# Quantiser's last periods on VectorE, and stage four's first quarter begun inside stage three

## The chip, the cores and the metric

One core of a Trainium2 chip runs the whole program. The metric is the device time of one execution in microseconds, the median over several runs. Every other time here comes from one profiled execution of the kernel.

## What is computed

The input `x` has shape (16, 32, 32, 32). Four stages follow each other, each adds to `x` a function of the normalised `x` (`_gn`: mean and variance over the 32x32 pixels of one channel):

```python
x = x + _L0_conv_ref(_gn(x), codebooks)      # residual quantiser: 8 codebooks of 512 rows of 32
x = x + _L1_conv_ref(_gn(x), ...)            # 1x1 and 3x3 convolutions, products of 8x8 patch spectra
x = x + _L2_conv_ref(_gn(x), ...)            # four directional scans, 31 dependent steps each
x = x + _L3_conv_ref(_gn(x), ...)            # snake convolution: offsets, sampling, normalisation
```

The two that the change touches, in short:

```python
def stage(res, cb):                          # quantiser, one codebook
    d = sum(res * res) - 2.0 * einsum('ne,ke->nk', res, cb) + sum(cb * cb)
    q = cb[argmin(d)]
    return (res - q, q)
...
off = conv2d(x, w_off, b_off, (1, 1), 'SAME')          # snake convolution, 3x3, 18 offsets
off = tanh(group_norm(off, g_gn_off, b_gn_off, K))
y_off_new = running sums of off outwards from the centre
out = conv2d(bilinear samples of x at y + y_off_new, w_dsc, ...)
out = relu(group_norm(out, g_gn, b_gn, 8))
```

## The kernel before

`x` stays in SBUF for the whole program as `X`, 128 partitions (four images x 32 channels) x 4 quarters of 1024 pixels. A quarter is `j`; half a quarter (512 columns) is a unit. Each stage is one function (`block_l0` to `block_l3`) that writes out the program of each engine by hand, with semaphores between engines. A stage ends in a barrier of all engines. Ahead of each stage stands a small block of its own, `prime`, in which SyncE (SP) increments every semaphore of the stage once (so that waits can be written as `START + n` with `START = 1`); a second barrier ends it.

**The quantiser, `block_l0`.** There are 64 periods: 8 codebooks x 8 units, and 5 more periods in which the pipeline drains. For one period's unit: TensorE (PE) scores the codebook, VectorE (DVE) finds the best row (`find`, line 553, an index per pixel), the index is spread over partitions (PE L268, then ScalarE's cast `l_ib`, L391), GpSimd (POOL) and ScalarE (ACT) turn it into one-hot rows: of the 8 one-hots of a unit (four groups `g`, near and far chunk) POOL makes the four near ones (`near`, L444) and one far one (L467), ACT the other three (L358, L364). PE picks the row and its step with them (L277, bank `PICK`). DVE adds it to the residual (`l_res`, L579), POOL multiplies by the step (`l_product`, L479), PE sums (L325), ACT takes a sign (L397), POOL multiplies sign and step (`l_signed`, L453) and subtracts it from the residual (`l_res`, L461). `back(w, i, par, n)` names the unit that is `n` periods behind: `early` 1, `fresh` 2, `mid` 3, `done` 5. When all is drained DVE takes the eight residuals out of `X` (L590). The text below numbers the units of the last codebook 59 to 63 by their period.

**Stage three's end, `block_l2`.** After the last scan step PE moves the result back in two halves (L1083), and DVE adds it to `X` in eight instructions (L1185): four give the pixels of quarters 0 and 1, four those of quarters 2 and 3. SP has loaded stage four's weights long before.

**Stage four's beginning, `block_l3`.** DVE takes statistics of quarter 0 (L1625, L1628, L1630), writes it normalised into `l_xz` (padded rows) and once more into `l_xe` (L1634), and then does the same for quarters 1 to 3. SP gathers the shifted columns for the offset convolution: for a quarter 12 DMAs from SBUF to SBUF, each 32 partitions x 1154 columns (`l_xi`, L1307). PE runs the offset convolution of both halves (24 matmuls each half, L1336) in one bank, between them ACT copies the first half out (`l_raw`, L1478); DVE takes its moments (L1640, L1643), ACT the tanh (L1490), and ACT and DVE split the offsets in turn into three 16-bit parts (L1493, L1671, L1497, L1677, L1503). With them PE forms running sums (L1354), from which DVE makes the first `l_term` (L1705), and POOL adds terms (`l_isum`, L1609) for the rest of the stage. Meanwhile POOL makes `l_down` and `l_bend` of quarter 0 (L1588, L1593).

## Time and profile before

| | us |
|---|---|
| median of 3 runs | 1644.4 (1643.44 to 1646.78) |
| the profiled execution | 1646.22 |
| its span, first to last instruction | 1643.3 |
| PE, POOL, DVE, ACT busy | 1389.7, 1076.4, 1240.0, 977.5 |
| stage one ends, stage two begins | 882.4, 884.9 |
| stage two ends, stage three begins | 1116.1, 1118.1 |
| stage three ends, stage four begins | 1311.5, 1314.15 |

The last three rows are places on the span's time axis, which all times of the trace use. A stage's end is the end of its last arithmetic, a stage's beginning the start of the first instruction behind both barriers. The profiled execution takes 2.9 us more than its span; what lies outside the span is no part of the trace.

### The profile page before, as it was taken

Reading aid. Unit: us, or ns where it says so; the run is one execution under the profiler, and the core shown is the slowest. Engines: PE = TensorE matmul, PEld = TensorE weight load, DVE = VectorE, ACT = ScalarE, POOL = GpSimd, SP = SyncE. Lnnn points to the kernel's source line nnn. Section 1 sums busy time; section 2 is a strip of 40 time slices with the busy share of each in tenths; the row PEclk is TensorE's granted clock in tenths of the full one; section 3 lists DMA queues with packets and bytes.
Section 4 is the critical chain, followed back from the end, with each engine's and each line's share of the span. In section 5 each row is a group of like instructions: output and inputs, shape, how many; then the busy total and the mean of one; then the engine's idle time right before and its main releaser. Section 6 shows DMA issues by size and latency. Waiting matters only on the chain. (4 is left out here: it accounts for less than half of the span.)

```text
span 1643.3 us, 36454 instructions
## 1 busy us (share of the span) xinstructions
PE 1389.7 (85%) x11793; PEld 605.9 (37%) x11812; DVE 1240.0 (75%) x4975; ACT 977.5 (59%) x1652; POOL 1076.4 (66%) x783
## 2 busy tenths in 40 slices
PE   3999999999999999999982999985888738676675
PEld 1333333333333333333331777753656401111111
DVE  4899999999999899999975354444222357877786
ACT  2488888888888788888881444321000025656554
POOL 4579999989999899999994223232000049788786
PEclk9999999999999999999996999997999958897877
DMA  7000000000000000000002435501000031010000
GB/s 166 8 2 9 5 9 4 2 11 5 9 4 2 11 5 9 4 2 2 1 2 57 98 83 115 115 0 53 1 2 2 1 87 44 1 44 14 1 14 26
DMA packets 18468, 42.27 MB, mean 26 GB/s; under 512 B 6501, under 2 KB 8137, under 8 KB 18269
## 3 DMA queue, kind: packets, MB, share of 16 engines
q1 hardware_dynamic: 16540, 38.50, 10.4%
q8 instruction: 97, 1.59, 0.4%
q10 hardware_dynamic: 1728, 1.35, 0.4%
q14 instruction: 103, 0.84, 0.2%
HBM read 8.92 MB, written 2.10 MB: 7 GB/s over the span
## 5 line engine op out<-in xcount | busy, mean ns | idle before, releaser
L444 POOL TENSOR_SCALAR l_onehot<-l_ib,c_iota 128x512 bf16<-128x512 f16 x256 | 400.6, 1565 | 58.3 <-ACT l_ib L391 58.3
L553 DVE FIND_INDEX8 l_idx<-l_top,l_scored 128x8 uint32<-128x256 f32 x1024 | 419.7, 436 | 0.0
L254 PE MATMUL ps<-l_ct_slot,l_res 32*128 32x512 f32 x2048 | 411.6, 613 | 0.0
L570 DVE CUSTOM_DVE_ANT_0 l_scored<-ps,l_gain 128x256 f32<-128x256 f32 x1024 | 383.8, 432 | 18.4 <-ACT l_gain L373 17.5
L373 ACT ACTIVATE l_gain<-ps 128x768 f32<-128x768 f32 (+1 forms) x384 | 284.2, 740 | 117.2 <-PE ps L254 116.6
L1609 POOL TENSOR_TENSOR l_isum<-l_term 128x512 f32<-128x512 f32 x160 | 205.1, 1313 | 65.9 <-DVE l_term L1711 34.5
L277 PE MATMUL ps<-l_onehot,l_cbp_slot 128*32 128x512 bf16 x3072 | 214.6, 386 | 6.6 <-POOL l_onehot L444 3.3
L248 PE MATMUL ps<-l_csq,l_row_slot 32*128 32x512 bf16 x1024 | 155.3, 397 | 17.9 <-DVE l_csq L548 6.4
L1362 PE MATMUL ps<-l_isum,w_l_w_dsc 64*64 64x512 f32 x640 | 104.8, 723 | 69.8 <-POOL l_isum L1609 68.9
L254 PEld LDWEIGHTS ps<-l_ct_slot,l_res 32*128 32x128 f32 x2048 | 155.9, 194 | 11.7 <-issue 0.9
L1537 ACT ACTIVATE ps<-ps,w_l_minus 128x512 f32<-128x512 f32 x192 | 118.3, 663 | 67.3 <-DVE l_term L1711 50.2
L730 PE MATMUL ps<-l_wc,l_xi 100*128 100x192 f32 x768 | 133.5, 331 | 24.5 <-DMA l_xi<-l_xt 24.5
L391 ACT CAST l_ib<-ps 128x512 f16<-128x512 f32 x256 | 149.3, 583 | 0.0
L730 PEld LDWEIGHTS ps<-l_wc,l_xi 100*128 100x128 f32 x768 | 125.9, 192 | 37.5 <-issue 36.7
L358 ACT ACTIVATE l_away<-l_ib,c_minus_iota 128x512 f16<-128x512 f16 x192 | 139.6, 727 | 0.0
L364 ACT ACTIVATE l_onehot<-l_away,c_one 128x512 bf16<-128x512 f16 x192 | 138.9, 723 | 0.0
L268 PEld LDWEIGHTS ps<-c_ident,l_idx 128*128 128x128 f16 x1024 | 58.8, 99 | 200.6 <-ACT l_ib L391 140.5
L1711 DVE SCALAR_TENSOR_TENSOR l_term<-ps,l_bend 128x512 f32<-128x512 f32 x192 | 120.4, 682 | 11.7 <-ACT ps L1537 11.4
L1584 POOL COPY l_xe<-l_xe 128x128 f32<-128x128 f32 (+1 forms) x16 | 6.2, 422 | 184.4 <-DVE l_xe L1634 184.2
L277 PEld LDWEIGHTS ps<-l_onehot,l_cbp_slot 128*32 128x32 bf16 x3072 | 59.2, 95 | 148.3 <-issue 59.9
L248 PEld LDWEIGHTS ps<-l_csq,l_row_slot 32*128 32x128 bf16 x1024 | 37.7, 91 | 192.7 <-DVE l_top L570 102.2
L268 PE MATMUL ps<-c_ident,l_idx 128*128 128x128 f16 x1024 | 103.3, 224 | 2.0 <-ACT l_idx L387 1.3
(157 smaller groups left out, 1955.5 us busy)
## 6 DMA issues: line engine op xcount, KB each, us to landing
l_xi<-l_xt SPq DMA_DIRECT2D x48, 384.0 KB, 7.0
l_xi<-l_xz SPq DMA_DIRECT2D x48, 144.2 KB, 3.1
X<-in_x SPq DMA_DIRECT2D x16, 128.0 KB, 7.9
out<-X SPq DMA_DIRECT2D x16, 128.0 KB, 2.1
l_ct<-in_codes_t SPq DMA_DIRECT2D x4, 448.0 KB, 13.0
l_ct_slot<-l_ct SPq DMA_DIRECT2D x7, 256.0 KB, 2.3
l_cbp_slot<-l_cbp SPq DMA_DIRECT2D x8, 96.0 KB, 1.9
l_wt<-in_l_w SPq DMA_DIRECT2D x1, 768.0 KB, 3.9
```

Source lines behind the costliest of these rows:

```text
L248: pe.matmul(ps[:, at + n - FIRST[k], :], row_slot[rows, par, :], csq[rows, :], start=True, stop=False, skip_group_check=True)
L254: pe.matmul(ps[:, at + n - FIRST[k], :], res[rows, i, P * tt:P * (tt + 1)], ct_slot[rows, par, :], start=False, stop=True, skip_group_chec ...
L268: mm = pe.matmul(ps[:, SPREAD, P * tt:P * (tt + 1)], idx16[:, i % 2, n:n + 1].to_broadcast([P, P]), ident16[:], start=True, stop=True)
L277: mm = pe.matmul(ps[C * g:C * g + C, PICK, :], cbp_slot[:, par, kind, a, c, :], onehot[:, i % 2, g, c, :], start=(c == 0 and a == 0), stop ...
L358: nc.scalar.activation(away[:, n, :], ib16[:, i % 2, g, :], ACT.Abs, bias=minus_iota[:, 1:2]).then_inc(s_away, 1)
L373: nc.scalar.activation(gain[:, at:at + GROUPS[k], :], ps[:, at:at + GROUPS[k], PAIRED:], ACT.Relu).then_inc(s_gain, 1)
L391: nc.scalar.copy(ib16[:, vi % 2, k - 2, :], ps[:, SPREAD, :]).then_inc(s_ib, 1)
L444: nc.gpsimd.tensor_scalar(onehot[:, i % 2, g, 0, :], ib16[:, i % 2, g, :], iota[:, 0:1], None, ALU.is_equal).then_inc(s_near, 1)
L553: nc.vector.max_index(idx8[:, i % 2, n, :], top[:, i % 2, n:n + 1].to_broadcast([P, 8]), scored[:, WIDE * (k % 3) + n - FIRST[k], :]).then ...
L570: nc.vector.tensor_tensor_reduce(out=scored[:, WIDE * (k % 3) + m, :], in0=ps[:, WIDE * (k % 2) + m, :PAIRED], in1=gain[:, WIDE * (k % 2) ...
L730: mm = pe.matmul(ps[:, py % 2, HID * u:HID * (u + 1)], xi[:, ky, g, at:at + P], wc[:, ky, :], start=(ky == 0), stop=(ky == 2))
L1609: nc.gpsimd.tensor_tensor(isum[:, it % SUMS, :], term[:, t0, :], term[:, t0 + 1, :], ALU.add).then_inc(s_sum, 1)
```

## The change

1. **Drain of the quantiser.** POOL and ACT's one-hots leave the last five periods. DVE runs a new function `drain` there: it makes the remaining one-hots of unit 62 (six) and unit 63 (eight), and does the three POOL operations (`settle`: sign times step, residual minus that; and the product), with the removal of each residual from `X` (`leave`) put between. A new semaphore `s_last` counts DVE's one-hots.
2. **No `prime`** ahead of stages three and four: their semaphores count from zero, one barrier is left of two. Stages one and two keep theirs, and stage one has one semaphore more to prime.
3. **Quarter 0 of stage four is normalised in stage three**: after the four adds of the first half DVE takes its statistics and writes `l_xz`, with the other four adds around it, and SP issues its gather at the end of its program of stage three.
4. **The gather by halves**: every quarter's gather has 24 DMAs, 12 of 612 columns for the upper half of the convolution (semaphore `s_xi[0]`), then 12 of 542 for the lower.
5. **First quarter by halves in stage four**: the convolution's second half goes to another bank (`ACC`), and tanh, rounding and splitting run as two pieces of 512 columns. The copy `l_xe` of quarter 0 is made first in stage four, then the other quarters.

```diff
+LATE_HOTS = (G - 2 + G, G - 2 + G + 2 * G)
...
+                        if scoring or w == ALL:
+                            pe.wait_ge(s_near, START + v * G + G)
+                        else:
+                            pe.wait_ge(s_near, START + (ALL - 2) * G + 2)
+                            pe.wait_ge(s_last, START + LATE_HOTS[v - (ALL - 2)])
...
-            periods(pool, period, DRAIN)
+            periods(pool, period, 0)
...
-            periods(dve, period, DRAIN)
-            for i in range(UNITS):
+            def hot(v, i, g, c):
+
+                dve.wait_ge(s_ib, START + v * G + (g + 1))
+                nc.vector.tensor_scalar(onehot[:, i % 2, g, c, :], ib16[:, i % 2, g, :], iota[:, c:c + 1], None,
+                                        ALU.is_equal).then_inc(s_last, 1)
+
+            def settle(v, i):
+
+                dve.wait_ge(s_sign, START + v + 1)
+                nc.vector.tensor_tensor(signed[:], signed[:], step[:, i % KEPT, :], ALU.mult).then_inc(s_signed, 1)
+                dve.wait_ge(s_signed, START + v + 1)
+                nc.vector.tensor_tensor(res[:, i, :], res[:, i, :], signed[:], ALU.subtract).then_inc(s_res, 1)
+
+            def leave(i):
+
                 dve.wait_ge(s_res, START + ALL + i + 1)
                 xi = X[:, i * HALF:(i + 1) * HALF]
                 nc.vector.tensor_tensor(xi, xi, res[:, i, :], ALU.subtract).then_inc(s_out, 1)
+
+            def drain(w, i, scoring, par, use):
+                if scoring:
+                    return period(w, i, scoring, par, use)
+                early, fresh, mid, done = (back(w, i, par, n) for n in (1, 2, 3, 5))
+                if early:
+                    dve.wait_ge(s_top, START + early[0] * TILES + TILES)
+                    dve.sem_inc(s_alone, 1)
+                    find(early[1], SLOTS - 1)
+                if fresh:
+                    v, vi, vp = fresh
+                    for g in range(2 if early else 0, G):
+                        hot(v, vi, g, 0)
+                    for g in range(G):
+                        hot(v, vi, g, 1)
+                if done:
+                    settle(done[0], done[1])
+                if i == 0:
+                    for e in range(UNITS - DRAIN):
+                        leave(e)
+                if mid:
+                    v, vi, vp = mid
+                    dve.wait_ge(s_middle, START + v + 1)
+                    nc.vector.tensor_tensor(res[:, vi, :], res[:, vi, :], ps[:, PICK, :],
+                                            ALU.add).then_inc(s_off, 1)
+                    dve.wait_ge(s_off, START + v + 1)
+                    dve.wait_ge(s_product, START + v)
+                    nc.vector.tensor_tensor(product[:, vi % 2, :], res[:, vi, :], step[:, vi % KEPT, :],
+                                            ALU.mult).then_inc(s_product, 1)
+                if done:
+                    leave(done[1])
+
+            periods(dve, drain, DRAIN)
...
+def load_columns(sp, xz, xi, j, s_xi):
+
+    flat = xz[:, j].rearrange("p y x -> p (y x)")
+    for h, at in enumerate((slice(0, UPPER), slice(UPPER, SHIFTED))):
+        for g in range(G):
+            for kx in range(3):
+                sp.dma_start(xi[C * kx:C * kx + C, g, at],
+                             flat[C * g:C * g + C, kx + at.start:kx + at.stop]).then_inc(s_xi[h], 16)
...
-        prime(nc, semaphores)
...
+            sp.wait_ge(s_zero, START + 1)
+            sp.wait_ge(s_next_xz, START + 1)
+            load_columns(sp, xz, xi, 0, s_xi)
...
+            act.wait_ge(s_next, START + 3)
+            nc.scalar.activation(xstd[:, 0:1], xmv[:, 0:1, 1], ACT.Sqrt, bias=eps[:]).then_inc(s_next_std, 1)
...
+            for r in range(G):
+                add_output(0, r)
+            dve.wait_ge(s_out, START + G)
+            for h in range(2):
+                nc.vector.bn_stats(xstats[:, 0, h, :], X[:, h * HALF:(h + 1) * HALF]).then_inc(s_next, 1)
+            dve.wait_ge(s_next, START + 2)
+            nc.vector.bn_aggr(xmv[:, 0, :], xstats[:, 0]).then_inc(s_next, 1)
+            add_output(1, 0)
+            dve.wait_ge(s_next_std, START + 1)
+            nc.vector.reciprocal(xrstd[:, 0:1], xstd[:, 0:1]).then_inc(s_next, 1)
+            dve.wait_ge(s_next, START + 4)
+            dve.wait_ge(s_zero, START + 1)
+            nc.vector.tensor_scalar(xz[:, 0, 1:H + 1, 1:W + 1], X[:, 0:HW].rearrange("p (y x) -> p y x", x=W),
+                                    xmv[:, 0, 0:1], xrstd[:, 0:1], ALU.subtract, ALU.mult).then_inc(s_next_xz, 1)
+            for r in range(1, G):
+                add_output(1, r)
...
-            for j in range(J):
-                columns(j)
+            for j in range(1, J):
+                sp.wait_ge(s_xz, START + j)
+                sp.wait_ge(s_conv, START + 2 * j)
+                load_columns(sp, xz, xi, j, s_xi)
...
-                    if ky == 0 and h == 0:
-                        pe.wait_ge(s_xi, START + (j + 1) * (16 * 3 * G))
+                    if ky == 0:
+                        pe.wait_ge(s_xi[h], (j + 1) * (16 * 3 * G))
...
-            for h in range(2):
-                if h:
-                    pe.wait_ge(s_raw[0], START + h)
-                offset_conv(0, h, range(3))
+            offset_conv(0, 0, range(3))
+            offset_conv(0, 1, range(3), ACC)
...
+            halves = [slice(HALF * h, HALF * (h + 1)) for h in range(2)]
+            for at in halves:
+                nc.scalar.activation(off[:, at], raw[:, 0, at], ACT.Tanh, bias=gstat[:, 0, 5:6],
+                                     scale=gstat[:, 0, 4:5]).then_inc(s_first_rounded, 1)
+            for h, at in enumerate(halves):
+                act.wait_ge(s_first_rounded, START + h + 1)
+                nc.scalar.copy(rounded[:, at], off[:, at]).then_inc(s_first_rounded, 1)
...
+            normalise(0, xe[:, 0, MID:MID + H, MID:MID + W], s_xe)
+            for j in range(1, J):
+                for h in range(2):
+                    at = j * HW + h * HALF
+                    nc.vector.bn_stats(xstats[:, j, h, :], X[:, at:at + HALF]).then_inc(s_gn, 1)
+            dve.wait_ge(s_gn, START + 2 * (J - 1))
+            for j in range(1, J):
+                nc.vector.bn_aggr(xmv[:, j, :], xstats[:, j]).then_inc(s_gn, 1)
+            dve.wait_ge(s_std, START + 1)
+            nc.vector.reciprocal(rstd[:, 1:], std[:, 1:]).then_inc(s_gn, 1)
+            dve.wait_ge(s_gn, START + 3 * (J - 1) + 1)
+            for j in range(1, J):
+                normalise(j, xz[:, j, 1:H + 1, 1:W + 1], s_xz)
+                normalise(j, xe[:, j, MID:MID + H, MID:MID + W], s_xe)
```

Where instructions stand, before and after, at the three places that matter. First VectorE at the end of stage one; before, behind the last search:

```order
L553 MAX_INDEX l_idx<-l_top,l_scored 128x8 x4
L579 TENSOR_TENSOR l_res<-l_res,ps 128x512 x3
L590 TENSOR_TENSOR X<-X,l_res 128x512 x8
L74 UNCONDITIONAL_BRANCH
```

and VectorE there after the change (`L596` a one-hot, `L602` and `L604` the two operations of `settle`, `L610` a `leave`, `L634` the add of before's L579, `L638` the product):

```order
L560 MAX_INDEX l_idx<-l_top,l_scored 128x8 x4
L596 TENSOR_SCALAR l_onehot<-l_ib,c_iota 128x512 x6
L602 TENSOR_TENSOR l_signed<-l_signed,l_step 128x512
L604 TENSOR_TENSOR l_res<-l_res,l_signed 128x512
L610 TENSOR_TENSOR X<-X,l_res 128x512 x3
L634 TENSOR_TENSOR l_res<-l_res,ps 128x512
L638 TENSOR_TENSOR l_product<-l_res,l_step 128x512
L610 TENSOR_TENSOR X<-X,l_res 128x512
L596 TENSOR_SCALAR l_onehot<-l_ib,c_iota 128x512 x8
L602 TENSOR_TENSOR l_signed<-l_signed,l_step 128x512
L604 TENSOR_TENSOR l_res<-l_res,l_signed 128x512
L634 TENSOR_TENSOR l_res<-l_res,ps 128x512
```

The first add behind the search now stands behind six one-hots, a `settle` and three `leave`s; the second behind eight more one-hots and a `settle`. Next VectorE from the end of stage three into stage four, before:

```order
L1185 TENSOR_TENSOR X<-X,ps 128x16x32 x8
L989 UNCONDITIONAL_BRANCH
L1618 UNCONDITIONAL_BRANCH
L1625 BN_STATS l_xstats<-X 128x6 x2
L1628 BN_AGGR l_xmv<-l_xstats 128x2
L1630 RECIPROCAL l_rstd<-l_std 128x1
L1634 TENSOR_SCALAR l_xz<-X,l_xmv,l_rstd 128x32x32
L1634 TENSOR_SCALAR l_xe<-X,l_xmv,l_rstd 128x32x32
L1625 BN_STATS l_xstats<-X 128x6 x6
```

and the same place on VectorE after the change:

```order
L1253 TENSOR_TENSOR X<-X,ps 128x16x32 x4
L1259 BN_STATS l_xstats<-X 128x6 x2
L1261 BN_AGGR l_xmv<-l_xstats 128x2
L1253 TENSOR_TENSOR X<-X,ps 128x16x32
L1264 RECIPROCAL l_rstd<-l_std 128x1
L1267 TENSOR_SCALAR l_xz<-X,l_xmv,l_rstd 128x32x32
L1253 TENSOR_TENSOR X<-X,ps 128x16x32 x3
L1054 UNCONDITIONAL_BRANCH
L1695 UNCONDITIONAL_BRANCH
L1699 TENSOR_SCALAR l_xe<-X,l_xmv,l_rstd 128x32x32
L1706 BN_STATS l_xstats<-X 128x6 x6
```

Statistics and `l_xz` of quarter 0 moved ahead of the stage's barrier (the branches); `l_xe` and all of the other quarters stay behind it. Last SyncE over the same border, before (the second and third branch lead through the priming block):

```order
L1064 DMA w_l_stack<-in_l_stack 128x64
L989 UNCONDITIONAL_BRANCH
L57 UNCONDITIONAL_BRANCH
L56 UNCONDITIONAL_BRANCH
L1297 UNCONDITIONAL_BRANCH
L1307 DMA l_xi<-l_xz 32x1154 x48
L1315 DMA out<-X 32x1024 x16
```

and SyncE after the change:

```order
L1128 DMA w_l_stack<-in_l_stack 128x64
L1040 DMA l_xi<-l_xz 32x612 x12
L1040 DMA l_xi<-l_xz 32x542 x12
L1054 UNCONDITIONAL_BRANCH
L1376 UNCONDITIONAL_BRANCH
L1040 DMA l_xi<-l_xz 32x612 x12
L1040 DMA l_xi<-l_xz 32x542 x12
```

All 24 DMAs of quarter 0 now stand ahead of SyncE's branch, and so ahead of the barrier that ends stage three.

## Rows read from the trace of the kernel before

**Rows 1.** Chain that ended last, share of the span by line (page).

```profile
POOL l_isum L1609 10%; PE ps L1362 1%; PE ps L1336 1%; SPq L1307 0%; POOL l_bend L1593 0%; POOL l_down L1588 0%; DMA l_xi<-l_xz 0%; POOL X L1616 0%; PE ps L1324 0%; ACT l_raw L1478 0%; PE ps L1385 0%; DVE l_term L1705 0%; DVE l_term L1711 0%; DVE l_stats L1640 0%
```

**Rows 2.** Timeline, 848 to 886 us: start, duration, engine, line, [idle before, releaser].

```profile
851.12 0.43 DVE L553 FIND_INDEX8 l_idx<-l_top,l_scored 128x8 uint32<-128x256 f32 x1
...
856.49 0.69 ACT L397 ACTIVATE l_signed<-ps,c_minus_tiny 128x512 f32<-128x512 f32 x1 [0.30 <-PE ps L325]
...
861.02 0.69 DVE L579 TENSOR_TENSOR l_res<-l_res,ps 128x512 f32<-128x512 f32 x1 [6.17 <-PE ps L277]
...
864.75 0.69 ACT L397 ACTIVATE l_signed<-ps,c_minus_tiny 128x512 f32<-128x512 f32 x1 [2.72 <-POOL l_res L461]
...
866.25 1.47 PE L277 MATMUL ps<-l_onehot,l_cbp_slot 128*32 128x512 bf16 x12 [3.31 <-POOL l_onehot L444]
...
871.58 0.69 DVE L579 TENSOR_TENSOR l_res<-l_res,ps 128x512 f32<-128x512 f32 x1 [9.87 <-PE ps L277]
872.18 10.26 DVE L590 TENSOR_TENSOR X<-X,l_res 128x512 f32<-128x512 f32 x8
...
873.55 0.69 ACT L397 ACTIVATE l_signed<-ps,c_minus_tiny 128x512 f32<-128x512 f32 x1 [3.55 <-PE ps L325]
...
877.44 0.69 ACT L397 ACTIVATE l_signed<-ps,c_minus_tiny 128x512 f32<-128x512 f32 x1 [3.21 <-POOL l_res L461]
```

**Rows 3.** Line 444 alone, POOL's near one-hots: min/median/max ns, first and last start.

```profile
L444 POOL TENSOR_SCALAR l_onehot<-l_ib,c_iota x256: 1552/1564/1581, 69.9 to 864.6; 128x512 bf16<-128x512 f16 x128
```

**Rows 4.** Two lines of VectorE alone, the same columns.

```profile
L514 DVE TENSOR_SCALAR l_res<-X,l_mv,l_rstd x8: 529/544/830, 26.2 to 63.0; 128x512 f32<-128x512 f32 x8
```

```profile
L541 DVE CAST l_csq<-l_csq_left x1: 427/427/427, 25.7 to 25.7; 128x512 bf16<-128x512 f32 x1
```

**Rows 5.** SyncE's own barrier instructions between stages two and three, the same columns.

```profile
L617 SPq EVENT_SEMAPHORE  x1: 17/17/17, 1116.5 to 1116.5; - x1
```

```profile
L56 SPq EVENT_SEMAPHORE  x1: 17/17/17, 1118.0 to 1118.0; - x1
```

**Rows 6.** Timeline, 1303 to 1353 us, columns as in rows 2.

```profile
1302.71 0.35 DVE L1167 SCALAR_TENSOR_TENSOR l_columns<-ps,l_bias,l_columns 128x128 f32<-128x128 f32 x1 [0.98 <-PE ps L1105]
...
1306.63 4.87 DVE L1185 TENSOR_TENSOR X<-X,ps 128x512 f32<-128x512 f32 x8 [2.24 <-PE ps L1083]
1314.15 1.29 DVE L1625 BATCH_NORM_STATS2 l_xstats<-X 128x6 f32<-128x512 f32 x2 [2.65 <-PEq L56]
...
1316.24 0.81 DVE L1634 TENSOR_SCALAR l_xz<-X,l_xmv,l_rstd 128x1024 f32<-128x1024 f32 x1
1316.97 0.81 DVE L1634 TENSOR_SCALAR l_xe<-X,l_xmv,l_rstd 128x1024 f32<-128x1024 f32 x1
...
1327.26 5.35 PE L1336 MATMUL ps<-l_xi,w_l_w_off 96*32 96x512 f32 x24 [18.76 <-DMA l_xi<-l_xz]
...
1329.01 0.81 DVE L1634 TENSOR_SCALAR l_xe<-X,l_xmv,l_rstd 128x1024 f32<-128x1024 f32 x1
...
1339.60 0.21 DVE L1643 BATCH_NORM_AGGREGATE l_mv<-l_stats 128x2 f32<-128x12 f32 x1
...
1343.32 1.24 ACT L1490 ACTIVATE l_off<-l_raw,l_gstat 128x1024 f32<-128x1024 f32 x1
...
1351.28 1.89 DVE L1705 SCALAR_TENSOR_TENSOR l_term<-ps,l_down 128x512 f32<-128x512 f32 x3 [1.93 <-remote]
```

**Rows 7.** Chain of waits, 1300 to 1353 us, first and last gather of quarter 0 (start, duration).

```profile
1317.08 0.59 SPq L1307
...
1324.14 3.08 DMA l_xi<-l_xz
```

**Rows 8.** SyncE's other DMA issues, by line, columns as in rows 3.

```profile
L215 SPq DMA_DIRECT2D l_row_slot<-l_stage_row x7: 602/602/723, 70.5 to 647.9; - x7
```

```profile
L703 SPq DMA_DIRECT2D l_xi<-l_xt x48: 591/1910/2056, 891.7 to 1055.8; - x48
```

```profile
L201 SPq DMA_DIRECT2D l_cbp_slot<-l_cbp x8: 464/465/592, 31.5 to 682.0; - x8
```

More of the change, by code:

```diff
@@ L398, in period @@
                                              bias=const["minus_tiny"][:]).then_inc(s_sign, 1)
-                    if fresh:
+                    if fresh and scoring:
                         v, vi, vp = fresh
@@ L978, with block_l2 @@
 DIRS = 4
-def block_l2(nc, ps, X, io, const, w3, xz):
+def load_columns(sp, xz, xi, j, s_xi):
[5 more added lines that the diff above has]
+                             flat[C * g:C * g + C, kx + at.start:kx + at.stop]).then_inc(s_xi[h], 16)
+def block_l2(nc, ps, X, io, const, w3, ahead, s_xi):
+    START = 0
     ident, eps = const["ident"], const["eps"]
+    xz, xi, xstats, xmv, xstd, xrstd = (ahead[name] for name in ("xz", "xi", "xstats", "xmv", "std", "rstd"))
     with ExitStack() as ctx:
@@ L1179, in _, with add_output @@
                 scan(d, step)
-            for half in range(2):
+            def add_output(half, r):
                 dve.wait_ge(s_turned, START + 4 + half + 1)
-                for r in range(G):
-                    xj = X[:, HW * 2 * half:HW * (2 * half + 2)].rearrange("p (j y r x) -> p r j y x", j=2, r=G, x=W)
-                    src = ps[:, 2 * r + half, :].rearrange("p (j y x) -> p j y x", j=2, x=W)
-                    nc.vector.tensor_tensor(xj[:, r], xj[:, r], src, ALU.add).then_inc(s_out, 1)
+                xj = X[:, HW * 2 * half:HW * (2 * half + 2)].rearrange("p (j y r x) -> p r j y x", j=2, r=G, x=W)
+                z = ps[:, 2 * r + half, :].rearrange("p (j y x) -> p j y x", j=2, x=W)
+                nc.vector.tensor_tensor(xj[:, r], xj[:, r], z, ALU.add).then_inc(s_out, 1)
+            for r in range(G):
[14 more added lines that the diff above has]
+                add_output(1, r)
             dve.wait_ge(s_out, START + 2 * G)
@@ L1213, with block_l3 @@
 SHIFTED = (H + 2) * PADW - 2
+UPPER = (ROWS + 2) * PADW
 OWN = ((0, 1), (2, 3), (4, 5), (6, 7), (8,))
 L3_WEIGHTS = ("l3_w_off", "l3_avg", "l3_cols", "l3_sums", "l3_part_mask", "l3_minus", "l3_w_dsc", "l3_stack")
-def block_l3(nc, ps, X, io, const, w3, xz, out):
+def block_l3(nc, ps, X, io, const, w3, ahead, s_xi, out):
+    START = 0
     eps = const["eps"]
+    xz, xi, xstats, xmv, std, rstd = (ahead[name] for name in ("xz", "xi", "xstats", "xmv", "std", "rstd"))
     with ExitStack() as ctx:
@@ L1462, in _ @@
         def _(act):
-            for i, js in enumerate((range(1), range(1, J))):
-                act.wait_ge(s_gn[i], START + 3 * len(js))
-                nc.scalar.activation(std[:, js.start:js.stop], xmv[:, js.start:js.stop, 1], ACT.Sqrt,
-                                     bias=eps[:]).then_inc(s_std, 1)
+            act.wait_ge(s_gn, START + 3 * (J - 1))
+            nc.scalar.activation(std[:, 1:], xmv[:, 1:, 1], ACT.Sqrt, bias=eps[:]).then_inc(s_std, 1)
             nc.scalar.copy(ones[:], sums[:]).then_inc(s_ones, 1)
@@ L1477, in copy_raw @@
                         act.wait_ge(s_y, START + j)
-                nc.scalar.activation(raw[:, norm, HALF * h:HALF * (h + 1)], ps[:, SIDE, :], ACT.Identity,
+                bank = ACC if norm == 0 and j == 0 and h == 1 else SIDE
+                nc.scalar.activation(raw[:, norm, HALF * h:HALF * (h + 1)], ps[:, bank, :], ACT.Identity,
                                      bias=cols[:, 3 * norm:3 * norm + 1]).then_inc(s_raw[norm], 1)
@@ L1521, in _ @@
             group_std(0, 0)
-            offsets(0)
-            middle_part(0)
-            all_parts(0)
+            act.wait_ge(s_gs[0], START + GS)
+            halves = [slice(HALF * h, HALF * (h + 1)) for h in range(2)]
[5 more added lines that the diff above has]
+                nc.scalar.copy(rounded[:, at], off[:, at]).then_inc(s_first_rounded, 1)
+            for h, at in enumerate(halves):
+                act.wait_ge(s_first_left, START + h + 1)
+                nc.scalar.copy(rounded[:, at], left[:, at]).then_inc(s_first_rounded, 1)
+            for h, at in enumerate(halves):
+                act.wait_ge(s_first_left, START + h + 3)
+                nc.scalar.copy(parts[:, 0, at], off[:, at]).then_inc(s_off, 1)
             for p in range(PASSES):
@@ L1683, in _ @@
             gain_of(0, 0)
-            first_left(0)
-            second_left(0)
+            halves = [slice(HALF * h, HALF * (h + 1)) for h in range(2)]
+            for a, (src, dst) in enumerate(((off, left), (left, off))):
+                for h, at in enumerate(halves):
+                    dve.wait_ge(s_first_rounded, START + 2 * a + h + 3)
+                    nc.vector.scalar_tensor_tensor(out=dst[:, at], in0=rounded[:, at], scalar=part_mask[:, a:a + 1],
+                                                   in1=src[:, at], op0=ALU.mult, op1=ALU.add).then_inc(s_first_left, 1)
             for p in range(PASSES):
@@ L1882, in build_program @@
         w3 = {name: t("w_" + name, list(io[name].shape), F32) for name in L3_WEIGHTS}
-        xz = t("l3_xz", [P, J, H + 2, PADW])
-        block_l2(nc, ps, X, io, const, w3, xz)
-        block_l3(nc, ps, X, io, const, w3, xz, out)
+        ahead = {"xz": t("l3_xz", [P, J, H + 2, PADW]), "xi": t("l3_xi", [3 * C, G, (H + 2) * PADW]),
+                 "xstats": t("l3_xstats", [P, J, 2, 6]), "xmv": t("l3_xmv", [P, J, 2]),
+                 "std": t("l3_std", [P, J]), "rstd": t("l3_rstd", [P, J])}
+        s_xi = [ctx.enter_context(nc.semaphore("l3_xi_" + name)) for name in ("upper", "lower")]
+        block_l2(nc, ps, X, io, const, w3, ahead, s_xi)
+        block_l3(nc, ps, X, io, const, w3, ahead, s_xi, out)
 def kernel(**inputs):
```

77 lines of the change are left out of this document (25 added, 52 removed).

## Prediction

> **What bounds the kernel now.** I read the chain that ended last first: only its tail is kept, the running sums of stage four on POOL [rows 1]. The change touches nothing of that tail; it moves the point from which it starts. A kernel of four stages with barriers is bounded stage by stage, so I went to the three borders that the diff touches and read the timeline there.
>
> *End of stage one.* The last search ends at 851.55; from there the drain is a chain through POOL. Sign(60) ends at 857.18, the add of unit 62 starts 3.84 us later at 861.02 after an idle of 6.17, sign(61) comes at 864.75 because POOL's `l_res` was late, PE's picks of unit 63 at 866.25 because a POOL one-hot was late, so the add of unit 63 starts at 871.58 after 9.87 us without work on DVE [rows 2]. A POOL one-hot takes 1.56 us [rows 3]. Behind the add DVE takes eight residuals out of `X` in 10.26 us, of which the last waits for unit 63 (sign(63) at 877.44); the end is 882.44 [rows 2]. DVE, the idle engine, could do the same work: that is what the edit does.
>
> *Between stages two and three* the first barrier releases SP at 1116.5 and the second at 1118.0 [rows 5]: 1.5 us go into the priming block.
>
> *Stage three to four.* The eight adds run 1306.63 to 1311.50, statistics start 1314.15, `l_xz` is done at 1317.05. PE's first convolution waits for the gather, 18.76 us of idle ending at 1327.26; DVE meanwhile runs from `l_xe` of quarter 0 (1316.97) to the last `l_xe` (1329.82), 12.85 us. Moments are aggregated at 1339.60, tanh starts at 1343.32, the first term at 1351.28 [rows 6]. The gather is 12 issues from 1317.08 to 1324.14, 0.642 us apart, and the last lands 3.08 us behind its issue [rows 7].
>
> **The change part by part.** The profiled execution took 1646.22 with a span of 1643.3, 1.8 us over the median of the runs; I work out the change of the span and apply it to the median.
>
> *1. The drain.* New on DVE: 14 one-hots, and per unit two operations of `settle` and a product. An f32 tensor-tensor takes 0.69 [rows 2], taken as 0.70 with its wait; adds follow each other at 0.61 [rows 6], taken as 0.60 for a `leave`. DVE shows no one-hot (f16 in, bf16 out, a scalar per partition). The nearest rows: a 128x512 f32 tensor_scalar 0.544, a 128x512 cast into bf16 0.427 [rows 4]. Successive tensor_scalars start 0.08 closer than their length (0.81 long, 0.73 apart [rows 6]), so 0.46 and 0.35 apart; I take 0.40. Then: search ends 851.55; six one-hots to 853.95; settle(59) to 855.35 (its sign was long there); three leaves to 857.15; add(61) 857.15 (3 us later than needed, but its PE work is off the chain); PE's sum starts 0.8 later and the sign 1.14 after that, so sign(60) 859.1 to 859.8; eight one-hots fit before 862.2, settle(60) to 863.6; add(62) at sign(60)'s end plus the 3.84 of before, 863.6; sign(61) 865.5 to 866.2; add(63) 3.84 later, 870.1; sign(62), as before 1.97 behind the add [rows 2], 872.0 to 872.7; settle(62) to 874.15; sign(63) to 874.9; settle(63) to 876.3; last leave 877.05. Against 882.44: **-5.4**. The first seven leaves are hidden in waits. With one-hots 0.46 apart the same list gives -4.55, with 0.67 (no faster than an f32 tensor-tensor) -1.6, with 0.35 -5.7. The bound below: the whole chain from sign(62) on costs what it costs.
>
> The Trainium skill ("VectorE: DVE Perf Modes", the perf-mode tier table) says that a tensor_scalar with all tensors 16-bit in SBUF runs in a mode four times the base rate; as an estimate from that page one one-hot every 0.27 us, and the drain -6.2. No trace so far shows such an instruction on DVE.
>
> One semaphore more is primed: 0.06 (1.5 us for 14 of them and a barrier [rows 5] bounds it at 0.11).
>
> *2. No priming.* Stages two to three: second release minus first, **-1.5** [rows 5]. Nothing else moves there: the first instruction follows a release as before. At stages three to four the saving is in the next sum.
>
> *3 and 4. Gather ahead.* DVE: four adds end at 1306.63 + 2.4 = 1309.05, two statistics 1.29 [rows 6], aggregate, one add, ACT's root in its cover, reciprocal, `l_xz` 0.81: done at about 1312.2, that is 4.85 earlier than 1317.05; the last three adds end at 1314.0, 2.5 later than before. But SP now issues 24 DMAs, and stands at the barrier only behind them (the order of SP shows the branch behind all 24). What does an issue cost? 148 KB took 0.59, and a DMA of 32 KB from SBUF to SBUF 0.602 [rows 7, 8]; so size does not set it, and half-size ones cost the same 0.64 apart. SP reaches the barrier at 1312.2 + 24 x 0.64 = 1327.5, and everyone is released at 1327.7 (a barrier takes about 0.2 from the last arrival to the release). Before, stage four's first instruction ran at 1314.15 [rows 6]. PE's convolution, at 1327.26 before, starts at 1327.85, 0.6 later; the upper half has landed by then (12th issue at 1319.3 plus 3.1), the lower lands near 1330, before it is asked for. With the other bank both halves run through to about 1337.9, where copying stood between them before.
>
> The Trainium skill ("DMA: Bandwidth & Descriptors", rules for kernel authors) speaks against the halving: small transfers should be joined into large ones, as they mostly pay overhead. The rows agree: 24 halves cost SP 15.4 us where 12 cost 7.7.
>
> The release hits DVE: 12.85 us of normalising (of it a POOL conflict, `l_xe` of quarter 1, that comes again, as POOL starts from `l_xe` of quarter 0 as before) now start at 1327.75 and end at 1340.6; the moments of the convolution stand behind them on DVE. Aggregated at about 1341.9 instead of 1339.60: **+2.3**. Before, this DVE work was hidden behind the gather.
>
> *5. Halves.* Tanh to first term took 7.96 [rows 6]: four ACT passes (tanh, 1.24, is one) and two of DVE over 1024 columns, one after another. By halves ACT and DVE overlap: an ACT pass of 512 is 0.69 [rows 2], and so is a DVE one of that size in f32; chain tanh, tanh, round, left, round, left, parts of 512 with 0.04 between, then the old 0.9 to the first term: 5.3. **-2.65**. First term at 1341.9 + 3.7 + 5.3 = 1350.9 against 1351.28: stage four's start **-0.4**, and POOL's sums go on from there as before. Quarters 1 to 3 gather with 24 issues too, under the long sums: hidden.
>
> Sum: -5.4 + 0.06 - 1.5 - 0.4 = **-7.3**, 1637.1.
>
> **The rivals.**
> (a) *Issues are cheaper when half as large.* l_cbp_slot's issues (96 KB, SBUF to SBUF) took 0.465 [rows 8], about 0.5 apart: the barrier is reached 3.4 earlier, all of DVE's work too. Total -10.7: 1633.7. Against it the 32 KB row at 0.602.
> (b) *SP waits at the block's end for its transfers to land*: the barrier comes 2.5 to 3 later, and with it moments and first term. Total -4.5: 1639.9. Before, SP never reaches a border with a transfer under way, so no row speaks for or against.
> (c) *One-hots on DVE at the f32 rate*, 0.67: drain -1.6, total -3.5: 1640.9. Against it the cast's 0.427 [rows 4].
> (d) *One-hots faster than either row of 512 columns*: as short as DVE's instruction of 128x128, 0.35 long [rows 6] and so 0.27 apart: drain -6.2, total -8.1: 1636.3. For it: nothing is read or written here in f32 but the scalar. Against it: the cast, with one side in 16 bit, is at 0.427. The rule of the Trainium skill above would end here.
> (e) *Slower.* SP's issues are held back, as those of stage two's gather were: 0.59 unblocked, 1.91 in the median [rows 8]. Every 0.1 us on an issue moves the barrier by 2.4 us, and DVE's work, moments and the first term with it. From 0.94 us apart the 7.3 are gone, from 1.08 the kernel is slower by over 0.2%; at 1.9 it would be +23. For it: those rows. Against it: they moved 384 KB per issue, here it is half of 148 KB, in the same spacing half of the rate at which rows 7 show no hold.
>
> **How the numbers follow.** The forecast as it stands (with one-hots 0.35 to 0.46 and DVE's queue as worked out): 0.52. (a) 0.11, (b) 0.10, (c) 0.06, (d) 0.13, (e) 0.05; 0.03 for things unseen. A measurement tells 0.2%, 3.3 us, from no change. All but (e), (c) in part and the unseen end faster by more: faster 0.85, same 0.10, slower 0.05. Likeliest time 1637.1. The range takes in (a), (b), (c) nearly: 1633.0 to 1641.0.
>
> **What would show it.** Right: DVE's one-hots 0.35 to 0.46 apart; last `leave` near 877; one barrier of 0.2 us; 24 issues 0.64 apart from about 1312 on the old axis (1305 on the new); all engines released behind the 24th; DVE working through to the moments, PE's convolution finished before; tanh to first term 5.3. Wrong: SP at the barrier before its DMAs are issued, or a `leave` that waits in the middle of the drain for PE; PE's clock, granted at half while its drain work has gaps, would stretch the 3.84 between sign and add.

## The result, and the profile after

| | before | changed |
|---|---|---|
| first comparison: median (lowest to highest, 6 runs each) | 1643.92 (1640.95 to 1646.78) | 1635.27 (1628.24 to 1638.99) |
| second: median (15 and 10 runs) | 1644.38 (1640.96 to 1648.36) | 1636.53 (1631.94 to 1642.58) |
| ratio, first and second | | 0.9943 [0.9916, 0.9969], 0.9953 [0.9939, 0.9966] |
| span of the profiled execution | 1643.3 | 1626.4, in the second 1637.3 |

The forecast was 1637.1, range 1633.0 to 1641.0, and the kernel is 8 to 9 us faster: inside. The two profiled spans of one and the same changed kernel differ by 11 us, so a span proves nothing here; stretches between events have to be compared. The table does that for three traces; each number is the distance between two rows of a timeline.

| stretch, us | before | changed | changed, second trace | forecast of the difference |
|---|---|---|---|---|
| first search to end of last search (quantiser) | 814.3 | 806.3 | 815.1 | 0 |
| to end of last removal (drain) | 30.9 | 25.9 | 25.9 | -5.4 |
| last removal to first statistics of stage two | 2.5 | 2.5 | 2.5 | 0.06 |
| those statistics to the last add of stage two | 231.2 | 231.4 | 231.9 | 0 |
| last add of stage two to stage three's first statistics | 2.16 | 0.63 | 0.63 | -1.5 |
| stage three's first statistics to the first add of the output (scans) | 188.4 | 187.0 | 186.9 | 0 |
| first add to aggregated moments | 33.0 | 36.2 | 36.1 | +2.3 |
| moments to the first `l_isum` | 13.05 | 11.04 | 11.04 | -2.65 |
| first `l_isum` to the end | 290.7 | 288.4 | 290.6 | 0 |

The quantiser's 806.3 and the last row's 288.4 are not there in the second trace: other executions, not the change. The other rows repeat within 0.5 us. In the order of [rows 2], the drain's timeline in the changed kernel:

```profile
843.25 1.65 DVE L596 TENSOR_SCALAR l_onehot<-l_ib,c_iota 128x512 bf16<-128x512 f16 x6
...
846.14 1.89 DVE L610 TENSOR_TENSOR X<-X,l_res 128x512 f32<-128x512 f32 x3
...
847.95 0.68 DVE L634 TENSOR_TENSOR l_res<-l_res,ps 128x512 f32<-128x512 f32 x1
...
848.78 1.10 PE L332 MATMUL ps<-l_product,c_block_ones 128*128 128x512 f32 x2 [1.48 <-DVE l_res L634]
...
849.88 2.19 DVE L596 TENSOR_SCALAR l_onehot<-l_ib,c_iota 128x512 bf16<-128x512 f16 x8
849.91 0.69 ACT L404 ACTIVATE l_signed<-ps,c_minus_tiny 128x512 f32<-128x512 f32 x1 [1.99 <-PE ps L332]
...
850.74 2.75 PE L279 MATMUL ps<-l_onehot,l_cbp_slot 128*32 128x512 bf16 x24 [0.87 <-DVE l_onehot L596]
...
855.71 0.69 DVE L634 TENSOR_TENSOR l_res<-l_res,ps 128x512 f32<-128x512 f32 x1 [2.33 <-PE ps L279]
...
866.41 0.69 ACT L404 ACTIVATE l_signed<-ps,c_minus_tiny 128x512 f32<-128x512 f32 x1 [1.55 <-DVE l_res L604]
...
868.59 0.69 DVE L610 TENSOR_TENSOR X<-X,l_res 128x512 f32<-128x512 f32 x1
```

Eight one-hots end in 2.19 us: 0.27 each, where POOL took 1.56 [rows 3]. Nothing waits for a one-hot any more. The 0.87 us that the row of the picks at 850.74 puts down to one is the time of sign(60), which ended at 850.60: these picks write the bank that it reads, and wait for it; their own one-hots, unit 62's, were done at 844.90. The last removal ends 25.9 us behind the last search (843.34). But between sign(60), ended at 850.60, and the add at 855.71 lie 5.11 us, not 3.84: PE's 24 picks took 2.75 us, where 24 took 1.48 in the drain otherwise. In the granted clock of the stretches (busy times of PE, PEld, DVE, ACT, POOL; then the clock, third column from the right) one sees why; the changed kernel ahead of the sum of unit 60, and from 850.34 to 853.34:

```profile
847.34:848.84 1.50, 0.06 (x1) 0.09 (x1) 1.47 (x4) 0.58 (x1) 0.00 (x0) 1.00 0.00 0
...
850.34:851.84 1.50, 1.10 (x12) 0.54 (x16) 1.50 (x7) 0.26 (x1) 0.00 (x0) 0.50 0.00 0
851.84:853.34 1.50, 1.50 (x16) 0.37 (x8) 1.47 (x3) 0.00 (x0) 0.00 (x0) 0.50 0.00 0
```

The clock stands at half, 1.2 GHz, in the picks. Ahead of the sum, at 848.78, PE had stood idle for 1.48 us (the 0.06 us of the first row are the sum's own beginning).

At the border of stages three and four the barrier's own instructions of the changed kernel (VectorE's and SyncE's arrival, then SyncE's release):

```profile
L1054 DVEq DRAIN  x1: 17/17/17, 1298.5 to 1298.5; - x1
L1054 SPq DRAIN  x1: 368/368/368, 1312.2 to 1312.2; - x1
L1054 SPq EVENT_SEMAPHORE  x1: 17/17/17, 1312.7 to 1312.7; - x1
```

VectorE arrives at 1298.5; SyncE, behind its 24 issues, at 1312.2. The timeline there, as in [rows 6]:

```profile
1290.81 2.48 DVE L1253 TENSOR_TENSOR X<-X,ps 128x512 f32<-128x512 f32 x4 [2.23 <-PE ps L1150]
...
1295.65 0.81 DVE L1267 TENSOR_SCALAR l_xz<-X,l_xmv,l_rstd 128x1024 f32<-128x1024 f32 x1 [0.17 <-DVE l_rstd L1264]
...
1296.91 38.92 SPq L1040 DMA_DIRECT2D l_xi<-l_xz  x48
...
1312.85 7.80 PE L1406 MATMUL ps<-l_xi,w_l_w_off 96*32 96x512 f32 x48 [20.17 <-PEq L1054]
1312.85 0.81 DVE L1699 TENSOR_SCALAR l_xe<-X,l_xmv,l_rstd 128x1024 f32<-128x1024 f32 x1 [14.59 <-PEq L1054]
...
1318.58 3.77 POOL L1670 TENSOR_TENSOR l_bend<-l_down 128x1520 f32<-128x1520 f32 x1
...
1318.98 3.92 DVE L1699 TENSOR_SCALAR l_xe<-X,l_xmv,l_rstd 128x1024 f32<-128x1024 f32 x1
...
1324.99 0.80 DVE L1699 TENSOR_SCALAR l_xe<-X,l_xmv,l_rstd 128x1024 f32<-128x1024 f32 x1
1325.72 1.27 DVE L1720 BATCH_NORM_STATS2 l_stats<-l_raw 128x6 f32<-128x512 f32 x2
1327.02 0.21 DVE L1723 BATCH_NORM_AGGREGATE l_mv<-l_stats 128x2 f32<-128x12 f32 x1
...
1330.94 1.52 ACT L1591 ACTIVATE l_off<-l_raw,l_gstat 128x512 f32<-128x512 f32 x2
...
1336.69 4.87 DVE L1789 SCALAR_TENSOR_TENSOR l_term<-ps,l_down 128x512 f32<-128x512 f32 x8 [0.84 <-PE ps L1424]
```

PE and DVE both wait for the barrier (`PEq L1054`), 20.2 and 14.6 us, and no longer for the gather. The convolution is over at 1320.65; the moments come at 1327.02, straight behind DVE's last `l_xe`. Counted from the first add, the first `l_term` comes 45.9 us later, against 44.7 before: the border has become longer by 1.2 us.

### The profile page after: what moved, and what is told of

Same layout as the page of the kernel before. It is cut to its first block and busy times, and to the rows that moved or that the text cites. A ratio compares the mean times of both kernels' runs of the same rounds, so it can differ in the third digit from the quotient of the medians.

```text
span 1626.4 us, 36441 instructions
## 1 busy us (share of the span) xinstructions
PE 1381.0 (85%) x11812; PEld 602.1 (37%) x11812; DVE 1246.0 (77%) x5004; ACT 969.8 (60%) x1644; POOL 1045.9 (64%) x762
## 5 line engine op out<-in xcount | busy, mean ns | idle before, releaser
L451 POOL TENSOR_SCALAR l_onehot<-l_ib,c_iota 128x512 bf16<-128x512 f16 x250 | 390.7, 1563 | 51.3 <-ACT l_ib L398 51.3
L560 DVE FIND_INDEX8 l_idx<-l_top,l_scored 128x8 uint32<-128x256 f32 x1024 | 412.8, 418 | 0.0
L256 PE MATMUL ps<-l_ct_slot,l_res 32*128 32x512 f32 x2048 | 404.5, 603 | 0.0
L577 DVE CUSTOM_DVE_ANT_0 l_scored<-ps,l_gain 128x256 f32<-128x256 f32 x1024 | 376.7, 414 | 11.2 <-ACT l_gain L380 10.4
L365 ACT ACTIVATE l_away<-l_ib,c_minus_iota 128x512 f16<-128x512 f16 x186 | 135.2, 727 | 0.0
L371 ACT ACTIVATE l_onehot<-l_away,c_one 128x512 bf16<-128x512 f16 x186 | 134.5, 723 | 0.0
## 6 DMA issues: line engine op xcount, KB each, us to landing
l_xi<-l_xz SPq DMA_DIRECT2D x48, 76.5 KB, 2.1
l_xi<-l_xz SPq DMA_DIRECT2D x48, 67.8 KB, 2.0
```

What stands on the lines that cost most here:

```text
L256: pe.matmul(ps[:, at + n - FIRST[k], :], res[rows, i, P * tt:P * (tt + 1)], ct_slot[rows, par, :], start=False, stop=True, skip_group_chec ...
L365: nc.scalar.activation(away[:, n, :], ib16[:, i % 2, g, :], ACT.Abs, bias=minus_iota[:, 1:2]).then_inc(s_away, 1)
L451: nc.gpsimd.tensor_scalar(onehot[:, i % 2, g, 0, :], ib16[:, i % 2, g, :], iota[:, 0:1], None, ALU.is_equal).then_inc(s_near, 1)
L560: nc.vector.max_index(idx8[:, i % 2, n, :], top[:, i % 2, n:n + 1].to_broadcast([P, 8]), scored[:, WIDE * (k % 3) + n - FIRST[k], :]).then ...
L577: nc.vector.tensor_tensor_reduce(out=scored[:, WIDE * (k % 3) + m, :], in0=ps[:, WIDE * (k % 2) + m, :PAIRED], in1=gain[:, WIDE * (k % 2) ...
```

## The experiments

Every kernel was timed beside the kernel before on the same chip; differences in the text that follows are read from stretches, as above. A total has an interval of 2 to 7 us either way, so differences of a few us between two variants rest on the stretches of one trace each.

**The drain alone** (`drain_only`): the kernel before with the changed kernel's `block_l0`.

> Only the drain's part of the change: stages two to four as before, with both priming blocks. My theory (the drain's chain is shortened by VectorE's short one-hots, and lengthened by PE's half clock after the gap ahead of the sum of unit 60): from the end of the last search to the end of the last removal 25.9 us as in the changed kernel, against 30.9 before; the border between stages three and four as before (first add to aggregated moments 33.0 us); total about 5.0 us below the kernel before. Rival (the quantiser's scoring part is what got faster in the changed kernel's trace, by 8.2 us, through the change): here too the last search would end near 843 us, and the total would be 13 lower. If the scoring part only differs from run to run, the last search ends anywhere between 843 and 852.

1638.06 against 1644.58, ratio 0.9957 [0.9917, 0.9997]. The quantiser's scoring took 817.9 us here, more than before, and the last search ended at 855.6, outside the 843 to 852 expected: the 806.3 do not come with the drain. The drain took 24.66 and not 25.9, with the same instructions. The same stretches ahead of the sum and in the picks:

```profile
859.58:861.08 1.50, 0.07 (x1) 0.10 (x1) 1.47 (x4) 0.58 (x1) 0.00 (x0) 1.00 0.00 0
...
862.58:864.08 1.50, 1.10 (x24) 0.62 (x24) 1.50 (x7) 0.25 (x1) 0.00 (x0) 1.00 0.00 0
```

24 picks run in the time of 12, at the full 2.4 GHz, behind the same pause of PE; so the pause alone does not bring the half clock. Seven traces here have this drain program unaltered: three took 24.7, four 25.9, and in all four the clock stood at half there. The whole of the 1.27 us is this clock, and the program does not decide it. The old drain varies too. It took 30.9 us in the trace of before, where the clock stood at half from 866.2 to 869.6 while PE worked, and 32.7 in that of `no_prime` (below), where it stood at half from 864.8 to the drain's end.

**No gather in advance** (`no_ahead`): stage three as before but unprimed, quarter 0 normalised and gathered in stage four.

```diff
-            sp.wait_ge(s_next_xz, START + 1)
-            load_columns(sp, xz, xi, 0, s_xi)
...
-            for j in range(1, J):
+            for j in range(J):
```

> The changed kernel without its third part: quarter 0 is normalised and gathered in stage four, behind the one barrier that is left; drain, half gathers and half tanh stay. My theory (the 24 issues ahead of the barrier hold every engine, VectorE's normalising of the other quarters above all): without them that normalising is hidden behind the gather again, and from the first add of stage three's output to the aggregated moments it takes 31.5 to 32.5 us against 36.2 in the changed kernel and 33.0 before; total 4 us below the changed kernel. Rival (the gather in advance is worth what its transfers take): the moments come 4 us or more later than in the changed kernel, 40 us behind the first add.

1629.69, ratio 0.9898 [0.9876, 0.9921]. First add to moments 32.10, against 36.2 with the advance. So the third part of the change, with 24 half DMAs, costs 4.1 us. Timeline:

```profile
1299.83 4.87 DVE L1248 TENSOR_TENSOR X<-X,ps 128x512 f32<-128x512 f32 x8 [2.23 <-PE ps L1146]
...
1317.55 5.35 PE L1388 MATMUL ps<-l_xi,w_l_w_off 96*32 96x512 f32 x24 [15.87 <-DMA l_xi<-l_xz]
...
1320.37 0.81 DVE L1683 TENSOR_SCALAR l_xe<-X,l_xmv,l_rstd 128x1024 f32<-128x1024 f32 x1
...
1325.06 5.35 PE L1388 MATMUL ps<-l_xi,w_l_w_off 96*32 96x512 f32 x24 [2.16 <-DMA l_xi<-l_xz]
...
1331.92 0.21 DVE L1715 BATCH_NORM_AGGREGATE l_mv<-l_stats 128x2 f32<-128x12 f32 x1
```

DVE is done with normalising 3.9 us before the second half of the convolution starts: it is hidden again, and the gather's halves (PE waits for both) are the bound.

**Whole DMAs** (`whole_gather`): 12 of 1154 columns for a quarter, still ahead of the barrier.

```diff
-    for h, at in enumerate((slice(0, UPPER), slice(UPPER, SHIFTED))):
-        for g in range(G):
-            for kx in range(3):
...
+    for g in range(G):
+        for kx in range(3):
+            sp.dma_start(xi[C * kx:C * kx + C, g, :SHIFTED],
+                         flat[C * g:C * g + C, kx:kx + SHIFTED]).then_inc(s_xi[0], 16)
```

> The changed kernel, but each quarter's gather is 12 DMAs of 1154 columns instead of 24 halves. My theory (an issue costs 0.64 us whatever its size, and the barrier waits for the issues alone): SyncE reaches the barrier 7.7 us earlier, the convolution waits for the last landing some 1.5 us behind the release, VectorE's normalising still ends last: first add to aggregated moments 28.6 us against 36.2, total 7.6 below the changed kernel. Rival (issue time goes with size, or transfers hold the barrier until they land): 12 whole DMAs take as long as 24 halves, no difference.

1631.27, ratio 0.9894 [0.9859, 0.9929]; moments 28.53 us behind the first add, as worked out. An issue costs the same for twice the columns, and the barrier waits for issues, not for landings: in its timeline DVE starts at 1314.31, while PE still waits for the DMA. With 12 whole DMAs the gather in advance is worth having: 28.53 us, against 32.10 without it (`no_ahead`, in halves) and 31.6 in `no_prime` (12 whole ones behind the barrier, the convolution as before). It is the 24 issues ahead of the barrier that cost.

```profile
1314.31 0.81 DVE L1698 TENSOR_SCALAR l_xe<-X,l_xmv,l_rstd 128x1024 f32<-128x1024 f32 x1 [6.91 <-PEq L1053]
...
1316.23 7.14 PE L1405 MATMUL ps<-l_xi,w_l_w_off 96*32 96x512 f32 x48 [14.42 <-DMA l_xi<-l_xz]
```

**Two engines issue** (`split_gather`): the twelve in lots of three, in this order in the diff: SyncE and ScalarE ahead of the barrier, SyncE and ScalarE behind it.

```diff
+            for n in range(0, 3):
+                column(sp, xz, xi, 0, n, s_xi)
...
+            for n in range(6, 9):
+                column(act, xz, xi, 0, n, s_xi)
...
+            for n in range(3, 6):
...
+            for n in range(9, 12):
```

> As the one with 12 whole DMAs, but quarter 0's twelve are issued by two engines: SyncE three and ScalarE three ahead of the barrier, and three each behind it. My theory: the barrier falls at about 8.5 us behind the first add (VectorE's last add), the last DMA lands 13 us behind it, VectorE's normalising ends at 21.5, the convolution at 21.5 to 22; moments aggregated 23 us behind the first add against 36.2: total 13 below the changed kernel. Rival (both engines' issues share one path, or their transfers slow each other): landing no earlier than with SyncE alone, moments at 28 to 29.

1627.7, ratio 0.9897 [0.9871, 0.9923]; moments at 25.2, half-way between theory and rival. The barrier fell as expected (normalising over 21.6 us behind the first add), but the last DMA landed no earlier than with SyncE alone: the convolution started at 16.4, as at 16.3 there. The DMA view of 1303 to 1318 (busy tenths of the 16 engines, then median us from issue to landing):

```profile
DMA  0000004959999999999899999991000000000000
...
l_xi<-l_xz ACTq DMA_DIRECT2D x6, 144.2 KB, 4.7
l_xi<-l_xz SPq DMA_DIRECT2D x6, 144.2 KB, 4.4
```

With one engine the landing took 3.0, and the 16 engines were seven to nine tenths busy. Here the 1.77 MB move as fast as they can, some 10 us from the first issue to the last landing, and issuing them faster only makes them wait. The total is some 8 to 9 us below the changed kernel's, where 13 were expected.

**No priming, alone** (`no_prime`): the kernel before, with `START = 0` and without `prime` in stages three and four.

> The kernel before with one thing changed: no priming block ahead of stages three and four, whose semaphores count from zero. My theory (the block costs its increments and a barrier, and its pause also keeps PE's clock at half for longer when the scans begin): 1.5 us less between stages two and three, 2.1 less between stages three and four, and the scans, from stage three's first statistics to its first add, 187.0 us instead of 188.4, as in every trace without that block so far; total 5.0 below the kernel before. Rival (the 1.4 us in the scans come from something else in the change, such as where quarter 0 is normalised): the scans take 188.4 here, total 3.6 below.

1639.85, ratio 0.9974 [0.9956, 0.9993], 4.6 us. Between stages two and three -1.5; the scans 186.8; normalising over 2.1 earlier. Of these 2.1 only 1.4 reach the moments. The scans' gain is one of clock. The stretch from 14 to 17 us behind stage three's first statistics, before:

```profile
1132.24:1135.24 3.00, 2.88 (x28) 2.48 (x26) 0.35 (x1) 0.00 (x0) 2.02 (x1) 0.50 0.00 0
```

and without the priming block:

```profile
1131.49:1134.49 3.00, 2.44 (x41) 1.95 (x38) 0.70 (x2) 0.00 (x0) 2.02 (x1) 1.00 0.00 0
```

With 1.5 us less pause ahead of it this part of the scan is at the full clock. All ten traces of kernels without that block have 186.8 to 187.0, both with it 188.4. That it is the pause which moves the clock, and not chance as in the drain, rests on these two traces.

**The bend later** (`bow_later`): POOL's `l_bend` of quarter 0 behind its edge copies of all quarters.

```diff
                 if j == 0:
                     slope(0)
-                    bow(0)
+            bow(0)
```

> The changed kernel, with POOL's bend of quarter 0 moved behind its edge copies of quarters 1 to 3, so that it no longer runs beside VectorE's normalising. My theory (VectorE's l_xe of quarter 1 takes 3.9 us instead of 0.8 only because that POOL operation runs, and VectorE's queue is what the moments wait for): first add to aggregated moments 33.1 us against 36.2, total 3.1 below the changed kernel. Rival (the long instruction waits for something else, or POOL's later bend is needed sooner): the moments as in the changed kernel, or first term later.

1633.77, ratio 0.9933 [0.9913, 0.9954]; moments at 32.98 instead of 36.2, and the first `l_isum` no later behind them (10.9 us, 11.0 in the changed kernel). The total is not clear of the changed kernel's. The `l_xe` of quarter 1 in the changed kernel above took 3.92; here:

```profile
1323.97 0.80 DVE L1699 TENSOR_SCALAR l_xe<-X,l_xmv,l_rstd 128x1024 f32<-128x1024 f32 x1
```

The instruction itself is short; it was held up while POOL worked on `l_bend` (1318.58 to 1322.35 above, the held `l_xe` from 1318.98 to 1322.90). The Trainium skill ("SBUF — State Buffer", who interferes with whom) has VectorE and GpSimd sharing one pair of SBUF ports as an exclusive lock; this pair of rows, 3.92 and 0.80, agrees.

**The removals later** (`leaves_later`), three of them ahead of the add of unit 62, and spread (`leaves_spread`), one there and two ahead of unit 63's, the latter on top of the version with two issuing engines, at the end of this section.

```diff
-                if i == 0:
+                if i == 1:
                     for e in range(UNITS - DRAIN):
                         leave(e)
```

> The changed kernel, with the first three removals of the drain moved from ahead of the add of unit 61 to ahead of the add of unit 62, where VectorE waits anyway. My theory (the add of unit 61 was on the chain, and PE's pause before it sometimes lets the clock fall): last search to last removal 22.8 us, against 24.7 with the full clock and 25.9 with the half clock, and no stretch at half clock; total 2 to 3 below the changed kernel. Rival (as my prediction had it, that add is off the chain): 24.7 or 25.9 as before.

1636.88, ratio 0.995 [0.9929, 0.9972], no clear difference in time from the changed kernel; the drain took 23.52, 1.1 to 2.4 less, at full clock. The add of unit 61 was on the chain. It missed 22.8; that three removals did not fit the wait was the guess that `leaves_spread` put to the test.

**All together** (`two_queues`): 24 halves by two engines, the bend later, the removals later.

> All of it together: the removals later, the bend later, and quarter 0's 24 half DMAs issued by SyncE and ScalarE, three each ahead of the barrier and the rest behind it (upper halves first). My theory: barrier 8.7 us behind the first add, convolution from 12, VectorE's normalising ends at 18.6, lower half landed at 18.5, moments aggregated at 23.7 (36.2 in the changed kernel, 25.2 with whole DMAs by two engines); drain 22.8; total 14 to 15 below the changed kernel. Rival (landing is set by how fast the 1.77 MB move and not by the issues, as with the whole DMAs, whose convolution started at 16.3 to 16.4 with one engine or two): upper half no earlier than 15, moments at 25.

1622.47, ratio 0.9872 [0.9832, 0.9913]. Normalising over at 19.2, moments at 23.43. The convolution:

```profile
1312.71 4.79 PE L1419 MATMUL ps<-l_xi,w_l_w_off 96*32 96x512 f32 x24 [12.04 <-DMA l_xi<-l_xz]
...
1317.95 2.78 PE L1419 MATMUL ps<-l_xi,w_l_w_off 96*32 96x512 f32 x24 [0.45 <-DMA l_xi<-l_xz]
```

It starts 13.9 us behind the first add (1298.82): the rival, with no start before 15, fell, but 12 was too early: of the upper half the last issue of either engine took about 2 us (2.13 and 1.88) instead of 0.6, and landed 3.8 us behind its start. The convolution ends 21.9 us behind the first add, against 23.7 in `split_gather`, and in both the moments follow 1.5 us later. Half gathers pay once SyncE's issues no longer bind.

**The removals spread** (`leaves_spread`), on top of that version:

> As the version with two issuing engines, a later bend and later removals, but of the drain's first three removals one stands ahead of the add of unit 62 and two ahead of that of unit 63. My theory (three of them, 1.9 us, filled the wait of 1.3 us ahead of the add of unit 62 and ran 0.6 over): last search to last removal 22.9 us instead of 23.5; all else as there, total about 1622. Rival (PE's picks, not the removals, set that add): 23.5 again.

1620.04 against 1644.38, ratio 0.986 [0.9842, 0.9877]: 24 us faster than before and some 16 faster than the changed kernel. The drain took 23.00, near the 22.9 expected, so the removals had set that add.

**The change again** (`change_again`):

> The changed kernel unchanged, on the same chip as the version above, for a second trace and more times. My theory (the quantiser's scoring part varies by some 10 us between executions of any of these kernels; the drain takes 24.7 or 25.9, with or without a stretch at half clock): scoring part anywhere from 806 to 818, scans 187.0, first add to aggregated moments 36.2, total 1632 to 1640, about 8 below the kernel before. Rival (the 806 of the first trace belongs to the change): scoring near 806 again.

Its numbers stand in the tables above: scoring 815.1, drain 25.92, scans 186.9, moments at 36.1. The rival fell.

## Why the prediction was right

The sign, the size (-7.3 forecast, -8.65 and -7.85 measured), the drain and the priming between stages two and three were right. That the total fits is in part luck, for two misses offset each other: the first term of stage four was to come 0.4 us earlier, counted from the first add, and came 1.2 later; the scans, forecast at 0, gave 1.4. With the drain at -5.0 or -6.2 the stretches add up to -6.7 or -7.9.

- *Drain, -5.4 forecast.* Against the 30.9 of before's trace, measured -5.0 with the stretch at half clock, -6.2 without it; against the old drain's 32.7 in `no_prime`, up to -8.0. The term was sized with one-hots 0.40 apart; they are 0.27 apart, so rival (d) held, and the list of steps with 0.27 gives the -6.2. The rule of the Trainium skill ("VectorE: DVE Perf Modes", tier table) agrees: 0.348 us for one, 0.27 apart. The remark that the add of unit 61's PE work is "off the chain" was wrong, though the list itself counts on from that add: the sum of unit 60 stands behind it, and `leaves_later` gained 1.1 there. What I named as a danger at the end, PE's clock over the 3.84 us, happened in four of seven traces and costs 1.27.
- *No priming, -1.5.* Measured -1.53. Wrong was "Nothing else moves there": the scans gained 1.4 by the clock.
- *Gather in advance, +2.3 up to the moments.* The mechanism stood as written: SyncE holds the barrier, VectorE's normalising becomes the bound. The size was 3.2 (36.2 against 33.0): SyncE's first issue came 0.45 us behind `l_xz`'s end, not 0.03 as before, and release took 0.5 from SyncE's arrival, of which its own drain is 0.37, not 0.2. Working on to the moments took 14.2 us behind the release, as forecast. That it would have been better not done with half DMAs follows from `no_ahead`, 4.1 us; with whole ones it pays, by `whole_gather`.
- *Halves, -2.65.* Measured -2.2: from tanh to the first term 5.75 us, not 5.3. On the way from the moments to tanh the first of PE's two averages, 0.56 us at half clock instead of 0.35 at full, takes back 0.2.
- *Rivals.* (a) fell: issues of halves are 0.64 apart, in `whole_gather` 12 take half of 24's time. (b) fell: the release does not wait for landings. (c) fell. (e) did not come: each of the 24 issues took 0.58 to 0.67 us; with whole DMAs by two engines transfers did queue, but behind the issues, and with halves by two engines single issues were held for 2 us (`two_queues`).

The rule against many small DMAs ("DMA: Bandwidth & Descriptors", rules for kernel authors, in the Trainium skill) agrees for one issuing engine: the halves cost 7.7 us of SyncE, and 7.7 us at the moments. The Trainium skill puts mostly overhead under 64 KB, though, and the halves have 76.5 and 67.8 KB. With two engines halves were the better choice (13.9 against 16.4 to the convolution's start).

Why does scoring take 806 us in one execution and 812 to 818 in the others? Set beside the 806 of the changed kernel, the other traces lose their time in jumps: before's 5.6 us at 70 to 87 us and 2.2 near 550, others also up to 3 near 345. Near 345 and near 550 the jump is 1.4 to 3.3 us in just those traces whose granted clock stood at half there, and at most 0.2 in the rest. At 70 to 87 us before's clock is given as full, but six score matmuls took 1.85 us (at 82.90) where the changed kernel's took 1.02 (at 79.82). So the spread is, at least in the main, PE's clock. What stays open is why the clock falls in one execution and not in another; no run was made on it.

## What to carry to other kernels

Work issued ahead of a barrier delays all that stands behind the barrier: price what the other engines would have done in that time before moving a transfer forward (here 24 issues ahead of it lost 4.1 us, and 12 did not), and let the issues be few, or shared by two engines, or partly behind it. Where one trace of a kernel differs from the next by more than the change is worth, compare stretches between the same two events, in several traces. A pause removed can be worth more than its length if it shortens PE's time at half clock, so read the granted clock on both sides of it.
